# Two GraphSAGE layers on one Trainium2 core: the two weight products as one seven-product block form, and the neighbour mean taken of their result

## What is computed

```
def _sage_conv(x, src, dst, Wl, bl, Wr, num_nodes):
    agg = segment_sum(x[src], dst, num_nodes)
    cnt = segment_sum(ones, dst, num_nodes)
    agg = agg / maximum(cnt, 1.0)[:, None]
    return agg @ Wl.T + bl + x @ Wr.T
h1 = relu(_sage_conv(h, src, dst, Wl1, bl1, Wr1, 512))
x  = x + _sage_conv(h1, src, dst, Wl2, bl2, Wr2, 512)
```

## Time and profile before

| what | value |
|---|---|
| median of 3 runs | 358.89 us (358.74 to 358.93) |
| the profiled execution | 359.0 us, span of its profile 357.2 us |
| PE busy | 349.4 us (98%) |
| DVE busy | 221.1 us (62%) |
| POOL busy | 109.8 us (31%) |
| ACT busy | 83.6 us (23%) |
| chain that ended last | PE 88%, DVE 9%, DMA 1%, ACT 1%, issue 1% |

### The profile page before, as it was taken

One profiled execution on the slowest core, in us unless ns is written; L12 is line 12 of the kernel. 1 busy time (PEld: TensorE's weight loads), 2 busy tenths in 40 slices (PEclk: granted clock), 3 DMA queues, 4 the chain that ended last, 5 costly groups with the idle time before them and its releaser, 6 DMA issues.

```text
span 357.2 us, 4379 instructions
## 1 busy us (share of the span) xinstructions
PE 349.4 (98%) x1643; PEld 245.6 (69%) x1643; DVE 221.1 (62%) x377; ACT 83.6 (23%) x183; POOL 109.8 (31%) x90
## 2 busy tenths in 40 slices
PE   8999999997999999999999999999999999999996
PEld 4459888783488888888888888644556575446542
DVE  5899999998798897944895402056862735221210
ACT  3556663414300000000001322311331721221000
POOL 5000000008599999999111110002110380000000
PEclk9999999999999999999999999999999999999999
DMA  7100004159400000140200597730150000000001
GB/s 238 56 3 2 3 2 166 72 159 337 152 0 2 0 1 0 59 178 2 88 0 2 182 168 182 123 52 0 29 91 0 2 2 0 0 0 2 29 29 59
DMA packets 43830, 22.07 MB, mean 62 GB/s; under 512 B 35552, under 2 KB 36064, under 8 KB 43808
## 3 DMA queue, kind: packets, MB, share of 16 engines
q1 hardware_dynamic: 43280, 20.85, 21.0%
q0 software_dynamic: 240, 0.79, 0.7%
q10 hardware_dynamic: 288, 0.13, 0.1%
HBM read 20.72 MB, written 1.05 MB: 61 GB/s over the span
## 4 chain that ended last, share of the span: by engine, by line
PE 88%; DVE 9%; DMA 1%; ACT 1%; issue 1%; ACTq 0%
PE bank L1370 28%; PE bank L1482 14%; PE bank L1427 14%; PE bank L1637 8%; PE bank L1549 8%; PE bank L604 4%; PE bank L577 4%; PE bank L601 3%; PE bank L1358 2%; DVE h L1105 2%; PE bank L593 2%; DVE lo L1123 1%; DMA bias<-in_edge_type 1%; DVE stats L1053 1%; DVE h L1085 1%; DVE adj L1077 1%
## 5 line engine op out<-in xcount | busy, mean ns | idle before, releaser
L951 ACT ACTIVATE columns<-mean_var,eps 128x1 f32<-128x1 f32 x20 | 5.9, 294 | 130.0 <-DVE mean_var L1054 129.9
L1482 PE MATMUL bank<-slots,wall 128*128 128x256 f32 x128 | 30.2, 380 | 0.0
L1370 PE MATMUL bank<-wall,h_t 128*128 128x512 f32 x64 | 29.0, 594 | 0.8 <-ACT h_t L962 0.8
L1370 PE MATMUL bank<-slots,h_t 128*128 128x512 f32 x64 | 28.7, 594 | 0.8 <-ACT h_t L962 0.8
L873 POOL TENSOR_TENSOR spare<-slots 128x512 f32<-128x512 f32 x4 | 6.0, 1493 | 76.2 <-PE bank L1370 75.5
L1637 PE MATMUL bank<-wall,slots 128*128 128x512 f32 x64 | 28.4, 592 | 0.0
L1370 PE MATMUL bank<-h_t,spare 128*128 128x256 f32 x128 | 28.1, 379 | 0.0
L1549 PE MATMUL bank<-slots 128*128 128x512 f32 x64 | 27.8, 592 | 0.0
L604 PE MATMUL bank<-slots 128*128 128x112 bf16 x256 | 27.8, 228 | 0.0
L1482 PEld LDWEIGHTS bank<-slots,wall 128*128 128x128 f32 x128 | 24.2, 190 | 3.2
L1370 PEld LDWEIGHTS bank<-h_t,spare 128*128 128x128 f32 x128 | 24.2, 190 | 3.2
(11 more groups left out here) (223 smaller groups left out, 662.6 us busy)
## 6 DMA issues: line engine op xcount, KB each, us to landing
slots<-in_L_gnn_W_rel SPq DMA_DIRECT2D x4, 1024.0 KB, 11.0
spare<-in_L_gnn_W_ffn SPq DMA_DIRECT2D x1, 2048.0 KB, 8.0
slots<-in_L_gnn_W_ffn SPq DMA_DIRECT2D x1, 2048.0 KB, 8.6
slots<-in_L_gnn_Wl SPq DMA_DIRECT2D x32, 64.0 KB, 2.5
slots<-in_L_gnn_Wr SPq DMA_DIRECT2D x32, 64.0 KB, 2.5
x<-in_x SPq DMA_DIRECT2D x4, 256.0 KB, 6.4
bias<-in_L_gnn_W SPq DMA_DIRECT2D x2, 512.0 KB, 6.2
slots<-in_L_gnn_W_self SPq DMA_DIRECT2D x1, 1024.0 KB, 5.4
```

The costliest lines, as they stand in the source:

```text
L1370: ins = pe.matmul(bank, left, right, start=start and i == 0, stop=stop and i == len(pairs) - 1)
L1482: ins = pe.matmul(into, left[:, k, tile(p)], right[:, k, :], start=(n in (0, 2, 3, 5) and r == 0 and k == 0), stop=False, skip_group_check ...
```

## The change

Both layers now form `h @ [Wl | Wr]` at once: h (128-node tiles in pairs p = 0, 1) is split in node tile and in half of the features, the weights in half of the features and in l/r. Seven products P1 to P7 of 128 nodes by 256 features by 512 outputs (two float32 products each) give, after additions, `h @ Wl` and `h @ Wr` for both tiles of the pair. Then `means` multiplies the counts by `h @ Wl` (split into hi and lo), and the DVE multiplies each row by the in-degree's reciprocal and adds the own part and residual in one instruction. The degree is a column of four numbers per partition instead of a 128x512 tile, made by four one-column products.

POOL makes the weight differences (`combine_own`, four instructions of 128x1024 for a layer), the DVE the node sums (`sum_nodes`, four instructions of 128x256 for a pair) and the sums of products. ACT keeps P1 before P2 is added in the same bank, and makes `hi` of the result. The `turn`s of the second layer's weights move into the GCN part. The core of the diff (`made(p, n)` is the count after which product n of pair p is ready; two small helpers on ACT and the DVE, `keep_...` and `split_...`, make hi and lo):

```
 # setup
+SAGE_ORDER = [[P1, P2, P6, P7, P5, P4, P3], [P1, P6, P2, P7, P5, P4, P3]]
-sage_bank = [psum[6], psum[7], psum[2], psum[3]]
+sage_bank = [[psum[i] for i in row] for row in ((6, 7, 0, 1), (2, 3, 7, 6))]
 # POOL
+def combine_own(layer):
+    pool.wait_ge(turned[wl], KT)
+    pool.wait_ge(turned[wr], KT)
+    pool.tensor_tensor(t1, b12, b11, ALU.subtract).then_inc(wide_t_ready[layer], 1)
+    pool.wait_ge(wide_t_ready[layer], 1)
+    pool.tensor_tensor(t2, b22, t1, ALU.subtract).then_inc(wide_t_ready[layer], 1)
+    pool.tensor_tensor(b12, b22, b12, ALU.subtract).then_inc(wide_t_ready[layer], 1)
+    pool.wait_ge(wide_t_ready[layer], 2)
+    pool.tensor_tensor(t4, b21, t2, ALU.subtract).then_inc(wide_t_ready[layer], 1)
+def base(layer, p):
+    pool.wait_ge(upper_sum, done)
+    pool.tensor_tensor(own[:, 2 * p, :], sage_rows[p][1], add[0], ALU.add).then_inc(upper_based, 1)
+    pool.wait_ge(lower_sum, done)
+    pool.tensor_tensor(own[:, 2 * p + 1, :], sage_rows[p][2], add[1], ALU.add).then_inc(lower_based, 1)
+pool.wait_ge(down_ready, NT)
+combine_own(0)
 for t in range(NT): ... x += b2
+base(0, 0)
+combine_own(1)
+base(0, 1)
-for t in range(NT): ... lo[1] = h - hi[1]
 for t in range(NT): ... x += bl2
+pool.wait_ge(sage_biased, NT)
+for p in range(2):
+    base(1, p)
 # ACT
+for t in range(2):
+    root(TO_SAGE, t)
+    norm_relu(TO_SAGE, t)
+empty_h(H_SAGE1, 0)
+root(TO_SAGE, 2)
+norm_relu(TO_SAGE, 2)
+keep_first(0, 0)
+root(TO_SAGE, 3)
+empty_h(H_SAGE1, 1)
+norm_relu(TO_SAGE, 3)
 # DVE, GCN part, for half in range(2)
     for t in tiles:
         gcn_adjacency(t)
+    for k in range(KT):
+        turn(2 + half, k)
     for m in tiles: ... lo[0] of the GCN
 # DVE, GraphSAGE
+def sum_nodes(layer, p):
+    dve.wait_ge(t_out, use_of((H_SAGE1, H_SAGE2)[layer], 2 * p + 1) + 1)
+    dve.tensor_tensor(s1, a21, a22, ALU.add).then_inc(sage_s_ready, 1)
+    dve.wait_ge(sage_s_ready, made_so_far + 1)
+    dve.tensor_tensor(s2, s1, a11, ALU.subtract).then_inc(sage_s_ready, 1)
+    dve.tensor_tensor(a21, a11, a21, ALU.subtract).then_inc(sage_s_ready, 1)
+    dve.wait_ge(sage_s_ready, made_so_far + 2)
+    dve.tensor_tensor(s4, a12, s2, ALU.subtract).then_inc(sage_s_ready, 1)
+for layer in range(2):
+    sum_nodes(layer, 0)
+    for p in range(2):
+        if p == 0: split_upper(layer, p)
+        ... wait P6, first_kept;        upper = p6 + first          -> upper_sum
+        if p == 1: split_upper(layer, p)
+        ... wait P7;                    lower = p74 + upper         -> lower_sum
+        if p == 0: sum_nodes(layer, 1)
+        ... wait P5, lower_based;       own[2p+1] = p53 + own[2p+1] -> lower_own
+        ... wait P4;                    out_of_lower = p74 + upper  -> lower_out
+        split_lower(layer, p)
+        ... wait P3, upper_based;       own[2p] = p53 + own[2p]     -> upper_own
+    for m in range(NT):
+        own[m] = main[m] * inv_in[m] + own[m]                       -> sage_out[layer]
 # PE
+for n in SAGE_ORDER[p]:
+    P2 waits first_kept; P6 sage_s_ready 2, wide_t_ready 2; P7 sage_s_ready 3, wide_t_ready 3;
+    P4 lower_sum; P3 sage_s_ready 4, lower_own
+    sage_product(layer, p, n)
+    if n in between: fill_h(*between[n])
+sage_products(0, 0, {P1: fill tile 1, P6: fill tile 2, P7: fill tile 3}); sage_products(0, 1, {})
+means (fill 0 of the second layer after m = 2, fill 1 after m = 3)
+sage_products(1, 0, {P6: fill tile 2, P7: fill tile 3}); sage_products(1, 1, {}); means
 # degrees
-product(in_bank[:], [(ones[:], cnt_sum[:, 0, :])]).then_inc(cnt_ready, 1)
+for m in range(NT):
+    ins = product(deg_bank[:, NT + m:NT + m + 1], [(cnt_sum[:, 0, tile(m)], ones[:, 0:1])])
-link(dve.tensor_scalar(inv_cnt[:], in_bank[:], 1.0, None, ALU.max))
-dve.reciprocal(inv_cnt[:], inv_cnt[:]).then_inc(inv_cnt_ready, 1)
```

More of the change, by code:

```diff
@@ L731, in run_blocks, with made, wide @@
         sage_raw = [place(1), place(2), place(3), place(4)]
-        agg_t = [place(6), place(7)]
+        P1, P2, P6, P7, P5, P4, P3 = range(PRODUCTS)
+        SAGE_ORDER = [[P1, P2, P6, P7, P5, P4, P3], [P1, P6, P2, P7, P5, P4, P3]]
+        def made(p, n):
+            return PRODUCTS * p + SAGE_ORDER[p].index(n) + 1
+        def wide(n, i):
+            return slots[:, n, i * 2 * N:(i + 1) * 2 * N].rearrange("p (k n) -> p k n", k=2)
+        sage_t = [[wide(n, 0), wide(n, 1), wide(n + 1, 0)] for n in (6, 1)]
+        sage_rows = [[slots[:, n, i * N:(i + 1) * N] for i in range(4)] for n in (5, 0)]
+        narrow = [row[:, side[i]].rearrange("p (k n) -> p k n", k=2) for row in (b0[:], both_ways[:, 0, :], both_ways[:, 1, :]) for i in range(2)]
+        sage_s = [narrow[0:3], narrow[3:6]]
         def turned_rows(ap, quarter):
@@ L1507, in _ @@
             pe.wait_ge(wgt_deg_out, 1)
-            pe.wait_ge(inv_cnt_ready, 1)
             for n in range(PRODUCTS):
@@ L1582, in _, with sage_product @@
                     gcn(m, s)
-            def means(layer, exact):
[L1587 to L1592, removed]
-            for layer in range(2):
[L1595 to L1606, removed]
+            def sage_product(layer, p, n):
+                a11, a12, a21, a22 = (h_t[:, pair[i], tile(2 * p + j)] for j in range(2) for i in range(2))
+                b11, b12, b21, b22 = (wall[:, q, pair[i], :] for i in range(2) for q in (2 * layer, 2 * layer + 1))
+                s1, s2, s4 = sage_s[p]
+                t1, t2, t4 = sage_t[layer]
+                left, right = {P1: (a11, b11), P2: (a12, b21), P6: (s2, t2), P7: (a21, b12), P5: (s1, t1), P4: (a22, t4), P3: (s4, b22)}[n]
+                into = sage_bank[p][{P1: 0, P2: 0, P6: 1, P7: 2, P4: 2, P5: 3, P3: 3}[n]]
+                for k in range(2):
+                    ins = pe.matmul(into[:], left[:, k, :], right[:, k, :], start=(n in (P1, P6, P7, P5) and k == 0), stop=False,
+                                    skip_group_check=True)
+                ins.then_inc(sage_ready[layer], 1)
@@ new lines, in mean @@
+            def mean(layer, m, exact):
+                for q in range(NT):
+                    if m == 0:
+                        pe.wait_ge(out_lo, NT * layer + q + 1)
+                    for part in (hi[1 - layer], lo[1 - layer]):
+                        left, right = (cnt_r, part[:, q, :]) if exact else (wall[:, R], part[:, q, :].bitcast(F32))
+                        ins = pe.matmul(main[m][:], left[:, q, tile(m)], right, start=(q == 0 and part is hi[1 - layer]),
+                                        stop=(q == NT - 1 and part is lo[1 - layer]))
+                ins.then_inc(mean_ready[layer], 1)
@@ L1609, in _ @@
+            def means(layer, exact):
+                for m in range(NT):
+                    if m == 0:
+                        pe.wait_ge(upper_own, 2 * layer + 1)
+                    mean(layer, m, exact)
+                    if layer == 0 and m >= 2:
+                        fill_h(H_SAGE2, m - 2, sage_out[0])
+            for layer in range(2):
+                what, ready = ((H_SAGE1, h_ready[TO_SAGE]), (H_SAGE2, sage_out[0]))[layer]
+                pe.wait_ge(turned[2 * layer], KT)
                 if layer == 0:
-                    pe.wait_ge(adj_ready, 2 * NT)
@@ L1611, in _ @@
-                    own(0, 1)
-                    own(1, 2)
-                    fill_h(what, 3, ready)
-                else:
+                    pe.wait_ge(gcn_out, 2)
+                    transposed(what, 0)
+                    sage_products(0, 0, {P1: (what, 1, ready), P6: (what, 2, ready), P7: (what, 3, ready)})
+                    pe.wait_ge(gcn_out, NT)
+                else:
+                    transposed(what, 0)
+                    pe.wait_ge(upper_own, 2)
                     pe.wait_ge(sage_out[0], 2)
-                    for m in range(2):
-                        own(m)
-                        fill_h(what, m + 2, ready)
@@ L1619, in _ @@
[L1619 to L1623, removed]
+                    sage_products(1, 0, {P6: (what, 2, ready), P7: (what, 3, ready)})
                     pe.wait_ge(sage_out[0], NT)
+                transposed(what, 2)
+                sage_products(layer, 1, {})
+                pe.wait_ge(upper_sum, 2 * layer + 2)
                 with pe.If_eq(slow, 0):
@@ L1628, in _ @@
                     means(layer, False)
[L1629 to L1641, removed]
 _INS = ['x', 'src', 'dst', 'edge_type_4', 'edge_weight', 'L0_gnn_W', 'L0_gnn_b', 'L0_gnn_diffusion_weights',
```

160 lines of the change are left out of this document (105 added, 55 removed).

## The result

The changed kernel took 365.37 us, median of 4 runs (364.32 to 366.05), the kernel before 358.91 beside it (358.74 to 359.42). The ratio is 1.0175, 95% interval 1.0143 to 1.0207: slower, by 6.5 us. The forecast was 366.0 in a range of 361.0 to 368.5. The profiled execution took 366.03, span 364.1 against 357.2 before. PE is busy for less time (346.9 us against 349.4) and for a smaller share, DVE and POOL each for some 25 us more.

A forecast was written before the change was run, and what follows sets the result against it. PE bounds the kernel, busy 98% of the span, so removed products and added waits count in full. From 359.0, savings of 6.9 and 0.1 against added waits and clock cost, led by 7.6 at P3, gave 366.0 us, range 361.0 to 368.5.

The forecast's parts named there:

- All nine terms of the sum: Whole kernel: products -6.9, degree -0.1, GCN +1.0, P1 +1.3, P2 +0.6 and +1.0, P3 +7.6 and +0.7, clock +1.8 us.
- Rival C: First layer, pair 0: DVE keeps the port for a21 right behind s2; 363.5, or 361.7 with full clock; 10%.
- The saving of eight products: PE, both layers: 28 float32 products instead of 32 and so eight fewer in all, at 0.86 each, -6.9 us.
- rival B: POOL and DVE don't meet, so the eight saved products win: 354.9, or 356.6 if only combine_own(1) is missed; 16%.
- The long wait: First layer, pair 0: P3 waits for DVE sums held behind POOL's combine_own(1), +7.6 us.
- about 2.75 for the pair: Shared port: a 256-column DVE operation caught behind POOL's 128x1024 one costs about 2.75 us for both, instead of 0.4.
- The GCN collision: GCN tile 3: DVE's affine operations wait behind POOL's combine_own(0), 2.5 us late, making PE's transposes late, +1.0 us.
- P1's wait: First layer, pair 0: ACT does root and norm_relu of tile 1 before emptying tile 0, P1 starts later, +1.3 us.
- the two P2 waits: P2 waits for ACT's copy of P1: +0.6 us in the first layer, +1.0 in the second.
- Rival D: More goes wrong: second half-clock spell, late turns holding up the GCN, or base(0, 1) late; 368 to 370; 7%.
- Rival A: The P3 stall comes but PE's clock stays full: 364.2 us; 22%.
- The price of 1.8: PE behind the 7.6 us idle gap ahead of P3: clock falls, 3.6 us at half speed, +1.8 us.

The follow-up runs named there:

- experiment 1: Changed kernel with POOL's combine_own(1) moved after base(0, 1); 357.65 us, ratio to the kernel before 0.9963.
- experiment 2: Changed kernel with each of POOL's 128x1024 weight differences issued as two of 128x512; 361.38 us.
- experiment 6: Changed kernel with x + b2 first on POOL, then both layers' weight differences, all ahead of base(0, 0); 355.87 us, ratio to the kernel before 0.9910.
- experiment 3: Changed kernel with unused float32 products filling PE's gaps, two ahead of P1 and seven ahead of P3 of the first layer's pair 0; 362.77 us.
- experiment 4: Changed kernel with only the gap ahead of P1 filled by two unused float32 products, the gap ahead of P3 left; 364.75 us.
- experiment 9: Changed kernel with only ACT's order edited, transposed tile 0 emptied ahead of norm_relu of tile 1, POOL untouched; 365.12 us.
- experiment 7: Changed kernel with only combine_own(1) moved ahead of base(0, 0), combine_own(0) left in place; 356.63 us.
- experiment 8: On top of experiment 6, ACT empties transposed tile 0 ahead of norm_relu of tile 1; 355.73 us.
- experiment 11: On experiment 8 plus second-layer pair 0 order P1, P6, P2: first-layer P1 copy and tile 1 emptying earlier on ACT, node sums earlier on DVE; 354.36 us.

## Why the prediction was right

**The place and the mechanism.** All nine terms of the sum are found at the places named. P3 of pair 0 waited 6.8 us for three DVE sums that each stood behind one of POOL's 128x1024 operations; moving the call (experiment 1) removed that wait, halving POOL's instructions halved it (experiment 2). Rival C, a second DVE operation that keeps the port because it stands right behind, did not happen: a21 waited 2.56 like the others. The saving of eight products is real in full, 6.9 us; the form was never the trouble, and with POOL's work placed in its idle time it beats the kernel before by 3.1 us (experiment 6, 355.87). That is 1.0 above rival B's 354.9, which had left out the two short P3 waits of 0.5 that remain.

**What was mis-sized.** The long wait was put at 7.6 and is 6.8. The step that was off is "about 2.75 for the pair": 2.45 for POOL's operation and 0.3 for the DVE's turn. In the trace POOL's operations start 2.48 us apart on average (294.60 to 302.05, three steps). With the DVE out of the way the same three steps take 2.36 on average (last section), so POOL's part was 0.09 too large and the DVE's turn adds 0.12, not 0.3. Three times 0.27 is the 0.8. The GCN collision cost 0.7 instead of 1.0: the caught operation took 2.73 and the tile was 2.2 us late, not 2.5. P1's wait and the two P2 waits were each 0.1 to 0.3 too large.

**What was missed.** The half-speed spell at P1, 1.7 us, is in no part of the sum. Rival D named a second spell of half clock, at 7% and 368 to 370; it came in the profiled run and, by its mean clock of 0.986, in one more, and the two lie at 366 only because the waits were shorter than forecast. I took 0.84 us as the longest idle time that keeps the clock and priced only the 7.6 us gap; P1's gap of 1.82 us lies between, and in some runs the clock fell there. Without it the profiled run would have been near 364.3, where two of the four runs lie (364.32 and 364.71). So the closeness of 366.0 to the profiled 366.03 is partly two errors against each other: 1.7 missed, and 1.7 too much in the wait terms together. The forecast that the clock falls behind the long gap held in all four runs of the changed kernel (mean clock 0.986 or 0.991), and experiment 3 shows that the fall costs time. Rival A is out for that gap: two runs lie near its 364.2, but at 0.991, so they got there by shorter waits and not by full clock. The price of 1.8 is the changed kernel's profiled run; behind the same 6.67 us gap it was 2.0 in experiment 4's and 2.75 in experiment 9's. That it came out as forecast is partly luck. The Trainium skill's rule, TensorE: Matmul & The Clock Gate, "HAM oscillation — how this bites in real kernels", is that an idle gap in mid-kernel brings half speed. The traces agree for the gap of 6.67 us; behind 3.44 us the clock fell in the profiled run, but one of ten runs kept it.

**What stays open.** What decides whether the clock falls at P1. The profiled runs of the changed kernel and of experiment 1 are alike up to there, with the same 1.82 us gap and full clock in it, and the one fell and the other didn't. Experiments 1, 6 and the one with only the second gap filled, thirteen runs, show no fall. The profiled run of experiment 2 does (P1's four records took 3.43), and the mean clock of two runs of experiment 7 suggests it. That one kernel falls there more often than another is no more than a count of few runs. The length of the gap alone doesn't settle it. What sets the length of the spell behind the long gap is open too.

## What to carry to other kernels

Before work is handed to POOL in order to save PE, list the DVE operations with two SBUF inputs that will run at that time, and who waits for them: each is held for a whole POOL instruction, however short it is itself. Put POOL's long operations where the DVE reads PSUM or has nothing to do, or cut them, and prefer the cure of placement: here one moved call was worth 7.7 us on the medians (about 7 without the spells at P1), the eight saved products 6.9. A wait that stops PE for several microseconds cost 1.8 to 2.75 us more in clock here. A small idle time that was removed in one place came back in part at the next wait of the same engine's list, twice (experiments 8 and 11).

## What the runs showed of the hardware that was not expected

The clock fell to half speed behind an idle gap of 1.82 us (granted 0.54 for the following 3.74 us) after more than twenty microseconds of nearly unbroken matmuls, and in other runs did not. Against the 0.84 us of the kernel before, this is the shortest gap at which a fall was seen. Filling the two gaps with 7.7 us of unused products made the kernel 2.6 us faster.

The price of the spell behind the same 6.67 us gap was 1.8, 2.0 and 2.75 us in three profiles (the changed kernel, experiments 4 and 9), and the runs of experiment 4 differ by 1.3 us at the same mean clock of 0.991.

On the port, the DVE's turn almost disappears between two POOL operations: POOL's four 128x1024 operations of a layer started 2.48 us apart with a DVE operation between each two, against 2.36 without (experiment 6, POOL in order of time). POOL lost 0.12 us a turn, the DVE 2.1:

```profile
263.91 2.38 POOL L958 TENSOR_TENSOR slots<-wall 128x1024 f32<-128x1024 f32 x1
266.36 2.36 POOL L960 TENSOR_TENSOR slots<-wall,slots 128x1024 f32<-128x1024 f32 x1
268.68 2.37 POOL L961 TENSOR_TENSOR wall<-wall 128x1024 f32<-128x1024 f32 x1
271.00 2.38 POOL L963 TENSOR_TENSOR slots<-wall,slots 128x1024 f32<-128x1024 f32 x1
```
